# A two-layer cross-attention kernel: GpSimd makes a context's low half in four instructions, and adds a norm's bias rows behind the norm

## What is computed

```python
# layer 0, 16 heads of 32
x = layer_norm(h) ; q = x @ q_w + q_b ; k = ctx @ k_w + k_b ; v = ctx @ v_w + v_b
attn = softmax(where(mask, q @ k.T * scale, min))
h = h + (attn @ v) @ cproj_w + cproj_b
h = h + gelu(layer_norm(h) @ fc_w + fc_b) @ proj_w + proj_b
# layer 1: two attentions, 16 heads of 128, one extra bias key and value each; then an MLP of width 2048
for i in (1, 2):
    x = x + (softmax(q_i @ k_i.T / sqrt(128)) @ v_i) @ wo_i + bo_i
x = x + gelu(layer_norm(x) @ w_fc1 + b_fc1) @ w_fc2 + b_fc2
```

## Time and profile before

| | |
|---|---|
| median of 3 runs | 2556.66 us (2553.98 to 2557.16) |
| the profiled execution's own time | 2563.27 us |
| its span, first to last instruction | 2561.3 us |
| TensorE busy | 2436.5 us (95%) |
| VectorE busy | 1102.0 us (43%) |
| ScalarE busy | 1067.1 us (42%) |
| GpSimd busy | 559.2 us (22%) |
| mean granted TensorE clock | 0.973 of full speed |

### The profile page before, as it was taken

The page is one execution under the profiler, slowest core; times in us unless marked ns, Lnnn a source line. Parts: engine busy times, 40 slices in busy tenths (PEclk is TensorE's granted clock), DMA queues, the critical chain, the costliest instruction groups (busy, mean ns, idle before and its releaser), DMA issues.

```text
span 2561.3 us, 45887 instructions
## 1 busy us (share of the span) xinstructions
PE 2436.5 (95%) x14242; PEld 2170.8 (85%) x14242; DVE 1102.0 (43%) x2377; ACT 1067.1 (42%) x2551; POOL 559.2 (22%) x775
## 2 busy tenths in 40 slices
PE   5889988999999999999999989999999999999899
PEld 4667767988899899898998878998998998988798
DVE  5566655453233333333343442333333334344643
ACT  3455553234344444444444243444444444452321
POOL 4011113232022222222221230222212222122321
PEclk9899988999999999999999989999999999999899
DMA  5110011115211211212212443112112113214120
GB/s 159 54 33 17 19 38 31 52 54 157 84 58 58 91 58 47 83 58 80 80 64 64 137 128 113 58 47 83 58 58 91 50 46 99 68 51 146 38 66 29
DMA packets 196146, 179.48 MB, mean 70 GB/s; under 512 B 53758, under 2 KB 184242, under 8 KB 196018
## 3 DMA queue, kind: packets, MB, share of 16 engines
q1 hardware_dynamic: 196018, 177.97, 22.6%
HBM read 144.89 MB, written 33.05 MB: 69 GB/s over the span
## 4 chain that ended last, share of the span: by engine, by line
PE 83%; issue 7%; DVE 4%; POOL 3%; ACT 2%; DMA 1%; SPq 0%; POOLq 0%; ACTq 0%; DVEq 0%
PE ps_v L1045 9%; PE ps_v L1046 9%; PE ps_v L1047 9%; PE ps_k L1045 9%; PE ps_k L1047 8%; PE ps_k L1046 8%; PE ps_o L1155 7%; PE ps_t L1141 4%; PE ps_s L1045 4%; PE ps_s L1047 4%; PE ps_s L1046 4%; PE ps_o L1045 2%; PE ps_o L1047 2%; PE ps_o L1046 2%; PE ps_s L1120 1%
## 5 line engine op out<-in xcount | busy, mean ns | idle before, releaser
L864 DVE SCALAR_TENSOR_TENSOR k_lo<-ps_k,col_b,k_hi 128x375 fp32r<-128x375 f32 x256 | 155.6, 608 | 675.0 <-ACT k_hi L641 675.0
L520 POOL TENSOR_TENSOR cs_lo<-ctx_raw,cs_hi 128x1504 fp32r<-128x1504 f32 x72 | 247.8, 3442 | 736.3 <-DVE cs_hi L844 736.3
L1045 PE MATMUL ps_v<-w_b_hi,cs_hi 128*128 128x512 f32 (+1 forms) x928 | 393.7, 424 | 12.8 <-POOL w_b_lo L506 7.9
L1045 PE MATMUL ps_k<-cs_hi,w_a_hi 128*128 128x376 f32 x1152 | 389.9, 338 | 5.3 <-DVE k_lo L864 5.3
L1047 PE MATMUL ps_k<-cs_hi,w_a_lo 128*128 128x376 f32 x1152 | 386.3, 335 | 0.0
L1046 PE MATMUL ps_k<-cs_lo,w_a_hi 128*128 128x376 f32 x1152 | 385.5, 335 | 0.0
L1046 PE MATMUL ps_v<-w_b_lo,cs_hi 128*128 128x512 f32 (+1 forms) x928 | 367.4, 396 | 0.0
L1047 PE MATMUL ps_v<-w_b_hi,cs_lo 128*128 128x512 f32 (+1 forms) x928 | 367.0, 395 | 0.0
L641 ACT ACTIVATE k_hi<-ps_k,col_b 128x375 fp32r<-128x375 f32 x256 | 147.0, 574 | 423.4 <-PE ps_k L1047 412.1
L1155 PE MATMUL ps_o<-prob_t,v 128*128 128x112 f32 (+3 forms) x2304 | 241.8, 283 | 3.3 <-ACT prob_t L659 3.3
L1155 PEld LDWEIGHTS ps_o<-prob_t,v 128*128 128x128 f32 (+3 forms) x2304 | 230.2, 170 | 16.6 <-issue 16.6
(11 more groups left out here) (178 smaller groups left out, 4325.9 us busy)
## 6 DMA issues: line engine op xcount, KB each, us to landing
ctx_raw<-in_ctx_t SPq DMA_DIRECT2D x72, 752.0 KB, 4.4
w_raw_a<-in_blocks_a SPq DMA_DIRECT2D x104, 256.0 KB, 3.4
w_raw_b<-in_blocks_b SPq DMA_DIRECT2D x104, 256.0 KB, 3.5
q_lo<-q_scratch SPq DMA_DIRECT2D x72, 224.0 KB, 2.5
o_scratch<-o SPq DMA_DIRECT2D x64, 224.0 KB, 2.0
q_scratch<-prob SPq DMA_DIRECT2D x36, 224.0 KB, 2.7
q_scratch<-o SPq DMA_DIRECT2D x36, 224.0 KB, 2.8
cs_hi<-o_scratch SPq DMA_DIRECT2D x6, 672.0 KB, 4.2
```

The costliest lines, as they stand in the source:

```text
L520: pool.tensor_tensor(cs[place.parity][1][:, 0:DT * KW], ctx_raw[place.parity][:], cs[place.parity][0][:, 0:DT * KW], ALU.subtract).then_in ...
L864: dve.scalar_tensor_tensor(out=k[t % 2][1][:, 0:n], in0=ps_k[:, 0:n], scalar=cols(att)[:, ds(place.column((C_BK0, C_BK1), t), 1)], in1=k[t ...
L1045: pe.matmul(out, w_h, m_h, start=first, stop=False)
```

## The change

Two things move on GpSimd. `context_lo` makes the low half of a context in four instructions of 376 columns, where it was one of 1504; its semaphore `cs_lo` now counts four for a context, so the waits of TensorE and of the DMA queue on it are multiplied by `DT` = 4, and the DMA queue gets two further semaphore increments of its own. And in `ln` GpSimd first waits for the norm's last low half (`ln_lo`), then makes the pending weight block's low half, and then adds all seven bias rows. All other engines' instructions stay what they were.

```diff
@@ SyncE, load_context
-                wait(sp, cs_lo, place.batch - 1)
+                wait(sp, cs_lo, DT * (place.batch - 1))
+                sp.sem_inc(sp_waited, 1)
@@ GpSimd
             def ln(e, x0):
 
+                pool.wait_ge(ln_lo, RT * e + RT)
+                if has_pending(e):
+                    split_lo(*pending(e)[0:2])
                 pool.wait_ge(bias_in, 16 * e + 16)
                 for r in range(RT):
-                    pool.wait_ge(ln_xhat, RT * e + r + 1)
                     pool.tensor_tensor(x[:, r, :], x[:, r, :], bias_row[:], ALU.add).then_inc(bias_add, 1)
-                if has_pending(e):
-                    split_lo(*pending(e)[0:2])
 
             def context_lo(place):
                 pool.wait_ge(cs_hi, place.batch + 1)
-                pool.tensor_tensor(cs[place.parity][1][:, 0:DT * KW], ctx_raw[place.parity][:],
-                                   cs[place.parity][0][:, 0:DT * KW], ALU.subtract).then_inc(cs_lo, 1)
+                for c in range(DT):
+                    part = slice(c * KW, (c + 1) * KW)
+                    pool.tensor_tensor(cs[place.parity][1][:, part], ctx_raw[place.parity][:, part],
+                                       cs[place.parity][0][:, part], ALU.subtract).then_inc(cs_lo, 1)
@@ TensorE, context_ready
                     pe.wait_ge(cs_hi, place.batch + 1)
-                    pe.wait_ge(cs_lo, place.batch + 1)
+                    pe.wait_ge(cs_lo, DT * place.batch + DT)
```

## The result

The changed kernel takes 2511.09 us at the median of 4 runs (2509.85 to 2516.88), where the kernel before takes 2555.88 beside it (2553.98 to 2557.16): a ratio of 0.983 with a 95% interval of 0.9813 to 0.9847, or 44.8 us less. The forecast was 2508. In a second set of runs, the changed kernel's median was 2516.76 beside 2557.16, again 0.983 (0.9815 to 0.9845).

What follows compares the result with a forecast made beforehand. TensorE, busy 95% of the span, was taken as the bound, so only its pauses and lower-clock stretches counted. Layer 0's 28.5, norm 0's 7.5 and norms 1 to 4's 13.0 sum to 49.0 us: 2556.7 - 49.0 = 2508 us, range 2498 to 2523.

Steps and rivals of the forecast that it cites:

- The price of a piece: GpSimd's 376-column subtraction: 0.99 us each, bounds 0.84 and 1.14, 3.95 for four; a VectorE instruction waits one piece.
- GpSimd keeps the port through all four: Rival: VectorE waits through all four pieces, layer 0 loses 3.6 us, only the norms gain 20.5: 2540 us, chance 0.06.
- Layer 0, 28.5 us: Six attention pauses of TensorE fall from 3.08 to 0.7 us at full clock, batches to 33.2 us: 28.5 us gained.
- The part in batch 0: Layer 0's pause ahead of the five batch intervals: its shortening plus the lower-clock stretch behind it, 5.8 us gained.
- The clock falls all the same: Rival: layer 0's shorter pauses still lower TensorE's clock, so it gains 14 us, not 28.5: 2522 us, chance 0.12.
- 5.0 us a batch: In the rival on layer 0's clock: what a batch would lose in all, 3.1 us of it the pause.
- Norm 0, 7.5 us: Without bias rows delaying VectorE in norm 0, the 4.30 us pause and the half-clock stretch behind it go: 7.5 us gained.
- The wait that the change adds: Behind norm 0, bias rows and first contexts queue behind GpSimd's wait for `ln_lo`; hidden by the query, 3.9 us to spare.
- Norms 1 and 4, 2.4 us each: Last turn 4.5 us sooner, but bias rows land on the MLP's `hidden` halves: 2.4 us stay from each, 4.8 together.
- Norms 2 and 3, 4.5 and 3.7 us: VectorE no longer stretched in the norms; its work in the four queries behind has room for bias rows: 4.5 and 3.7 us.
- Slower: Rival: pieces above 1.65 us each hold back some 60 layer-1 batches; 2592 us at 2.0 a piece, chance 0.03.
- nothing: Rival: stalls replaced in full, by later `normalize` waits in layer 0 and by ScalarE in the norms: 2553 us, chance 0.03.

Runs made afterwards that it cites:

- the gate: Changed kernel, but in layer 0 GpSimd starts a context's pieces only when the batch's third tile is normalised: 2510.30 us, ratio 0.9806.
- bias rows late: Changed kernel, but in norms 1 and 4 GpSimd adds the bias rows only after the low halves of the MLP's first two chunks: 2508.33 us, ratio 0.9795.
- the gate and whole contexts: Changed kernel with the gate, and each context's low half one instruction again everywhere: 2520.33 us, ratio 0.9847.

## Why the forecast was right, step by step

*The price of a piece*, 0.99 us (0.84 to 1.14): 1.02 at the mean of 288, and four take 3.8 to 4.0 us in layer 1's batches. VectorE gets in behind the first piece, 1.17 us. (The forecast names three VectorE instructions that got between four of GpSimd's, where the earlier trace rows shows two. The third, a copy at 453.49, took 0.55 us, where the same copy takes 0.36 at 457.58.) By the Trainium skill (SBUF — State Buffer, "Who interferes with whom"), whoever starts first holds the shared ports for one whole instruction; the trace agrees, since the wait went from one GpSimd instruction of 3.36 us to one of 0.99 (91.56 to 92.55, the product out at 92.76), and fell as well to a middle value, 1.97 us at most, with two pieces. The rival that GpSimd keeps the port through all four is out.

*Layer 0, 28.5 us.* Pauses of 0.70 to 0.71 for the forecast 0.7, clock 1.00, five intervals 20.4 us shorter for 22.7. A batch takes 33.66 us, not 33.2: 0.5 us of it has no pause of its own, and most of that, 0.4 us over batch 6's 32.50, is still there when the gate has taken the 0.7 away; what it is stays open. The part in batch 0, 5.8 us, cannot be told apart in two pairs of profiles: from the first value product to batch 0's output it is 62.1 and 64.8 us before, 53.7 and 59.7 after, since a stretch at 1.2 GHz near 70 to 88 us comes and goes there. The pieces alone gave 27.0 us in total.

*The clock falls all the same* (2522): out at 0.7 us; at 1.5, in the two-piece kernel, it came true in one batch of six. (Its "5.0 us a batch" should be 4.75, a sixth of 28.5; the 2522 does not hang on it.)

*Norm 0, 7.5 us.* The first value product comes at 50.4 to 52.2 us in eleven profiles with the bias rows moved, and at 56.2 to 59.7 in three without: 6.5 us between the means, with 1.8 and 3.5 us of scatter inside the two groups. The pause of 4.30 is gone.

*The wait that the change adds.* Hidden, but by far less than the 3.9 us that were forecast. The bias rows took 12.3 us, 1.76 each, beside the weight low halves and context copies that VectorE makes there, where the forecast had carried over 1.47 each; the first context took 4.8 us and was done at 50.77, 1.2 us ahead of the first value product at 51.95. In the second profile it was done at 50.28, and TensorE stood 0.18 us and began at 50.53: here the new wait has just become the limit.

*Norms 1 and 4, 2.4 us each.* 1.9 and 1.75. The two terms of it were both short. The norm gives 4.8 us, not 4.5: from the first turn to the last tile's, norm 1 takes 8.85 us where it took 13.69. The collision takes back 2.9, not 2.1: the rest of the stage takes 20.6 us for 17.7. TensorE's pauses there sum to 3.05 us (0.65, 1.15, 1.25). Against a kernel in which nothing is in the MLP's way (bias rows late, 16.9) the collision costs 3.7.

*Norms 2 and 3, 4.5 and 3.7 us.* 5.95 and 4.7. The norms themselves give what was forecast: from the first turn to the last tile's, norm 2 takes 9.12 us for 13.53 and norm 3 11.43 for 15.13, so 4.4 and 3.7. What is wrong is the rest of the step. It said that VectorE's work in the queries has room, and it gave the contexts ahead of the attention nothing. With the move alone the turns are as short, and the rest of the two stages takes 2.9 and 2.8 us longer than before, so that 1.5 and 1.0 are left. With the pieces as well the rest is 1.5 and 1.0 us shorter than before, among other things because the pauses that the kernel before had there (0.41 and 0.65 us behind norm 2, 0.30 behind norm 3) are gone. The pieces without the move gained nothing there. So the move by itself uncovers a collision one stage on, and only the pieces keep it small. The totals alone would not have shown this: 27.0 + 13.2 = 40.2 us lies within the interval of both, 39.1 to 47.8 (2555.88 times one less the ratio's ends).

*The median.* The steps forecast 49.0, and the two sets of medians give 44.8 and 40.4. Layer 0's intervals are 2.3 us short of the forecast, norms 1 and 4 together 1.1 and norm 0 1.0, and norms 2 and 3 gave 2.4 more than forecast: that the misses partly cancel is luck. What is then left, 2.2 us in one set and 6.6 in the other, the runs cannot place, since the changed kernel's two medians differ by 5.7 themselves. The range's low end, 2498, was never near.

*Slower, and nothing*: the four pieces end in time in layer 1; an attention takes 812.4 us where it took 813.1.

## What to carry to other kernels

An instruction on an engine that shares a port is priced by its longest single piece at the moment when the other engine is on the path, not by its busy time: here GpSimd did 37 us more work and the kernel ended 45 us sooner. Look at what starts in the same 0.1 us, split it or shift its start. In layer 0 each alone was worth about the same (batches of 33.67 and 33.81 us, from 37.6 to 37.75), both together a little more (32.89), and both cost a few lines. When work is moved off a norm, follow it to where it lands, through the in-order queue of the DMA issuer too: a wait for a low half held back a store that stood behind it and had nothing to do with it. And look again at what the moved work now stands ahead of: the first context kept 1.2 us of cover in one profile and none in the other, where 3.9 had been forecast.

## What was not expected of the hardware

A pause of TensorE does not have one price, and its length alone does not set it. Behind 0.7 us the granted clock stayed at full speed in all six batches; behind 1.50 us it fell in one batch of six; behind 1.64 and 1.11 in a query it stayed. Behind 3.08 in every batch of four profiles, and behind 2.28, 2.37, 2.41 and 2.48 in a query, TensorE ran 3.4 us or more at 1.2 GHz; but behind 2.27, in the kernel with the gate and whole contexts, it stayed at 1.00 from 1475.63 to 1487.00. The same two pauses, 1.25 us and 0.8 us later 0.63, stand between 66 and 72 us in every profile with the bias rows moved, and between 72 and 79 in the others. The clock fell there in twelve of the fourteen, for 3.4 to 13.7 us, and in two, the first profile of the changed kernel among them, not at all. In three it fell within 0.1 us of the second pause's start, and in three more before that pause was over; that the second pause adds anything is not shown. So the same program differs from execution to execution: the kernel before was at 1.2 GHz from 79.2 to 86.0 us in one profile and from 74.4 to 88.1 in the next, with unchanged work around it, and in all for 137.2 and 139.9 us of its span; the changed kernel for 64.9 and 85.3. The kernel before scattered by 12 us over ten runs (2551.88 to 2564.11), so effects of 2 us could be read in stages and not in totals.

The wait is over with one GpSimd instruction, though the next stands right behind it. VectorE's 375-column product finished 0.2 us behind the first of four queued pieces, and beside GpSimd's 512-column bias rows VectorE's halves of the MLP took 1.42 and 1.54 us each, where they take 0.35 and 0.56 once the bias rows are moved away.
